# Blank rows written in the mixer, the experts' first rows and weights asked for in attention, four places for weights

## The reference, cut to what matters

```python
x = _layernorm(x + _L0_attn_ref(x, ...))              # a Mamba-2 mixer: projection, conv, scan, gate, projection
x = _layernorm(x + _L0_xattn_ref(x, ctx_1024, ...))   # attention of 16 heads over 77 context rows
x = _layernorm(x + _L0_ffn_ref(x, ...))               # 8 experts, each token to its best 2

def _L0_ffn_ref(x, gate_w, w1, b1, w2, b2, ln_g, ln_b):
    scores = xt @ gate_w
    ew, ei = jax.lax.top_k(scores, K)                 # K = 2, E = 8
    ew = jax.nn.softmax(ew, axis=-1)
    ...
    h = gelu(xt @ w1[e] + b1[e])                      # 256 -> 512
    o = h @ w2[e] + b2[e]                             # 512 -> 256
    y = _layernorm(xt + o, ln_g[e], ln_b[e])
    out = sum over the two experts of ew * y
```

## Time and profile before

| | us |
|---|---|
| median of 3 runs | 2362.49 (2360.77 to 2363.33) |
| the profiled execution, whole | 2369.48 |
| its span, first to last instruction | 2367.7 |
| TensorE busy | 2160.6 (91%) |
| VectorE busy | 1704.4 (72%) |
| ScalarE busy | 1444.5 (61%) |
| GpSimd busy | 1178.9 (50%) |
| moved by DMA | 262.02 MB, of it written to HBM 85.00 MB |

### The profile page before, as it was taken

One profiled execution on the slowest core, in us unless ns is written; L12 is line 12 of the kernel. 1 busy time (PEld: TensorE's weight loads), 2 busy tenths in 40 slices (PEclk: granted clock), 3 DMA queues, 4 the chain that ended last, 5 costly groups with the idle time before them and its releaser, 6 DMA issues. The chain is left out here.

```text
span 2367.7 us, 52943 instructions
## 1 busy us (share of the span) xinstructions
PE 2160.6 (91%) x15740; PEld 1921.0 (81%) x15741; DVE 1704.4 (72%) x4452; ACT 1444.5 (61%) x3032; POOL 1178.9 (50%) x1379
## 2 busy tenths in 40 slices
PE   6999999989896997999999999999958999999968
PEld 5887878878785887888888888888848999999934
DVE  6877777778775334776777677767755898888956
ACT  6777777777775335666666666666634444444425
POOL 2655556555564001343444343434333777777767
PEclk9999999999997998999999999999978999999965
DMA  4111111011110452222222222222226777777648
GB/s 147 49 31 35 36 35 35 31 35 35 35 31 23 169 210 88 72 85 79 78 70 73 73 81 70 73 69 85 83 84 227 232 238 235 237 237 244 226 162 288
DMA packets 167944, 262.02 MB, mean 111 GB/s; under 512 B 25068, under 2 KB 90100, under 8 KB 167860
## 3 DMA queue, kind: packets, MB, share of 16 engines
q1 hardware_dynamic: 153812, 224.26, 30.0%
q0 software_dynamic: 12960, 35.67, 4.0%
q10 hardware_dynamic: 1088, 1.07, 0.1%
HBM read 175.94 MB, written 85.00 MB: 110 GB/s over the span
## 5 line engine op out<-in xcount | busy, mean ns | idle before, releaser
L1551 ACT ACTIVATE b_wk_f<-b_ps_s,b_nmx 128x77 f32<-128x77 f32 x1024 | 233.7, 347 | 16.0 <-DVE b_nmx L1599 16.0
L604 DVE SCALAR_TENSOR_TENSOR a_conv<-a_xc_pad,a_cw,a_conv 128x256 f32<-128x256 f32 x384 | 219.4, 632 | 1.0 <-ACT a_conv L478 1.0
L2038 ACT ACTIVATE c_hid<-c_ps_h,c_b_c 128x256 f32<-128x256 f32 x284 | 111.4, 476 | 175.2 <-PE c_ps_h L114 112.5
L1559 ACT ACTIVATE b_pT<-b_ps_pT 77x1024 f32<-77x1024 f32 x128 | 130.6, 1021 | 142.3 <-PE b_ps_pT L1457 142.3
L112 PE MATMUL c_ps_o<-w,c_h_hi 128*128 x568 | 165.7, 292 | 23.4 <-DVE c_h_lo L2072 23.0
L2167 POOL DMA_INDIRECT made_scratch<-c_o_s,c_to x142 | 153.7, 1082 | 62.6 <-issue 32.5
L1615 DVE TENSOR_TENSOR k_wk_lo<-b_ps_oT,k_wk_lo 128x512 fp32r<-128x512 f32 x128 | 88.0, 687 | 128.5 <-ACT k_wk_lo L1565 128.5
L1542 ACT ACTIVATE b_qT<-b_ps_q,b_bq_s 128x256 f32<-128x256 f32 x256 | 107.5, 471 | 107.4 <-PE b_ps_q L114 106.3
L1843 POOL CAST w<-k_c_f 128x256 f32 (+1 forms) x32 | 14.0, 438 | 312.0 <-DMA k_c_f<-in_c_w 312.0
L112 PE MATMUL c_ps_h<-c_xT_hi,c_w 128*128 128x256 f32 x568 | 167.4, 295 | 0.0
L1445 PE MATMUL b_ps_s<-b_kz,b_qT 128*128 128x154 f32 x1024 | 156.2, 295 | 5.3 <-ACT b_wk_f L1551 5.3
(11 more groups left out here) (285 smaller groups left out, 7688.4 us busy)
## 6 DMA issues: line engine op xcount, KB each, us to landing
c_w<-parts_scratch SPq DMA_DIRECT2D x71, 1024.0 KB
c_xa<-sent_scratch SPq DMA_DIRECT2D x71, 260.0 KB, 4.5
d_got<-made_scratch SPq DMA_DIRECT2D x32, 512.0 KB, 4.9
keys_scratch<-k_k_s SPq DMA_DIRECT2D x8, 1232.0 KB, 4.7
b_kz<-keys_scratch SPq DMA_DIRECT2D x64, 154.0 KB, 2.8
b_vv<-values_scratch SPq DMA_DIRECT2D x32, 308.0 KB
a_xT_f<-in_xT SPq DMA_DIRECT2D x32, 256.0 KB, 3.1
a_x_f<-in_x SPq DMA_DIRECT2D x32, 256.0 KB, 2.7
```

The costliest lines, as they stand in the source:

```text
L604: dve.scalar_tensor_tensor(out=conv[:, m, :], in0=xc_pad[:, m, k:k + L], scalar=cw[:, m, k:k + 1], in1=conv[:, m, :], op0=ALU.mult, op1=AL ...
L1551: last = act.activation(pe_[:, u.par, c, :], s_scores[:, c // (C // GM), c % (C // GM), :], ACT.Exp, bias=nmx[:, u.par, c:c + 1])
L1559: act.activation(pT[:, u.par, :, :], ps_pT[0:LK, :, :], ACT.Copy).then_inc(s_pTc, 1)
L2038: last = act.activation(hid[:, T * m:T * m + T], ps_h[t.par][:, m // 2, T * (m % 2):T * (m % 2) + T], ACT.Gelu, bias=b1_c[:, t.par, m:m + 1])
```

## The change

Four things are altered.

1. **Blank rows.** The blank tile comes from the host as an input, `blank`. The mixer loads it once (item 0) and writes it over the *whole* of `routing.sent`, 271 tiles: with each of the items 0 to 29 three transfers of three tiles, and the last tile after the last step. SyncE then waits in the mixer until all have landed. Attention writes none any more: `fill_ends`, the copy to `free`, `nobody` and the operations on `none` go.
2. **First loads.** A new class `ExpertsHead` holds the places of the experts' rows and first weights, in memory that attention has done with, and the two loads. At the end of attention SyncE waits for the last projection and for the table (`TABLE_STEPS`), asks for weights 0, waits for the scatters, and asks for rows 0, rows 1, weights 1, rows 2, weights 2. The experts' stage begins with the third load ahead.
3. **Four places** for the first weights in place of two, asked for three tiles ahead, and in each step ahead of the rows.
4. **`send` on GpSimd** scatters first and then makes `pw` and `by_expert`. The TOKEN mark and the next count move to `exp_gap`, earlier in the item.

The diff, cut to its core:

```diff
@@ mixer_phase, SyncE
+            tiles, per_item = routing.TILES, 3
+            whole_items = routing.n_blank // (tiles * per_item)
+
+            def blank_rows(b):
+                if b.known() and b.value() == 0:
+                    routing.load_blank(sp)
+                    sp.wait_ge(routing.s_none, 16)
+                if not (b.known() and b.value() >= whole_items):
+                    for i in range(per_item):
+                        routing.blank_rows(sp, (b.value() * per_item + i) * (tiles * L), tiles)
...
-            run_steps(sp, n_seq, [(store, 3), (load_xT_ahead, 0), (load_x, 0), (load_following, 0)], spare=2)
+            run_steps(sp, n_seq, [(store, 3), (load_xT_ahead, 0), (load_x, 0), (load_following, 0), (blank_rows, 2)], spare=2)
+            done = whole_items * per_item * tiles
+            for first in range(done, routing.n_blank):
+                routing.blank_rows(sp, first * L, 1)
+            sp.wait_ge(routing.s_blank, 16 * (whole_items * per_item + routing.n_blank - done))
@@ Routing
+    def load_blank(self, sp):
+        sp.dma_start(self.none[:, :, :], self.blank).then_inc(self.s_none, 16)
+
+    def blank_rows(self, sp, first, tiles):
+        sp.dma_start(self.sent[bass.ds(first, L * tiles), :].rearrange("(k p c) d -> p k (c d)", p=P, c=NT),
+                     self.none[:, :, :].rearrange("p c d -> p (c d)").unsqueeze(1).to_broadcast([P, tiles, NT * WIDE])
+                     ).then_inc(self.s_blank, 16)
@@ ExpertsHead (new)
+    X = 8
+    W = 4
+
+    def __init__(self, nc, ctx, signals, weights, head, places):
+        self.w1 = [w[:, :, :].rearrange("p k n -> p (k n)")[:, 0:MF * 2 * D].rearrange("p (q h n) -> p q h n", q=MF, h=2)
+                   for w in places]
+        spans = ([weights.wk_f[:, :, :].rearrange("p k n -> p (k n)")] * 3 + [weights.w_stage[:, 2, :]] * 3
+                 + [head.c_f[:, :, :].rearrange("p k n -> p (k n)")] * 2)
...
+    def load_w1(self, sp, routing, b1, t):
+        e = sp.value_load(routing.table[0:1, 1, bass.ds(t.value(), 1)], min_val=0, max_val=E - 1)
+        sp.dma_start(self.w1[self.place(t)].rearrange("p k h n -> p k (h n)").bitcast(F32),
+                     routing.parts[bass.ds(MF * e, MF), :, :].rearrange("k p n -> p k n")).then_inc(self.s_w1_in[self.place(t)], 16)
+        sp.dma_start(self.b1_c[:, self.place(t), :], b1[bass.ds(e, 1), :, :].rearrange("o p m -> (o p) m")
+                     ).then_inc(self.s_w1_in[self.place(t)], 16)
+
+    def load_rows(self, sp, routing, t):
+        r = sp.value_load(routing.table[0:1, 0, bass.ds(t.value(), 1)], min_val=0, max_val=routing.sent.shape[0] - L)
+        sp.dma_start(self.xa[t.slot], routing.sent[bass.ds(r, L), :].rearrange("(c p) d -> p c d", p=P)
+                     ).then_inc(self.s_xa_in[t.slot], 16)
@@ attention_phase, SyncE
             sp.wait_ge(s_ahead, 16 * E)
-
-            sp.wait_ge(s_none, 3)
-            for i in range(E - 1):
-                sp.dma_start(tile_rows(E * routing.region + L * i), routing.none[:, :, :]).then_inc(s_blank, 16)
-            fill_ends(sp, 0)
-            sp.wait_ge(s_blank, 16 * (2 * E - 1))
+            sp.wait_ge(s_out, 4 * n_seq)
+            sp.wait_ge(s_tab, TABLE_STEPS)
+            experts_head.load_w1(sp, routing, b1, Item(0, 0, ExpertsHead.X))
+            for par in (0, 1):
+                sp.wait_ge(s_scat[par], 16 * 2 * NT * (n_seq // 2))
+            sp.wait_ge(s_pT, 4 * n_seq)
+            experts_head.load_rows(sp, routing, Item(0, 0, ExpertsHead.X))
+            for i in range(1, 3):
+                experts_head.load_rows(sp, routing, Item(0, i, ExpertsHead.X))
+                experts_head.load_w1(sp, routing, b1, Item(0, i, ExpertsHead.X))
@@ attention_phase, ScalarE and VectorE
-            fill_ends(act, E // 2)
...
-            dve.memset(routing.none[:, :, :], 0.0).then_inc(s_none, 1)
...
-                dve.tensor_copy(routing.free[:, :], base[0:1, :]).then_inc(s_free, 1)
@@ attention_phase, GpSimd
                 pool.tensor_tensor(e2[:, :], euler[:, :], gap[:, :], ALU.pow).then_inc(s_e2, 1)
...
+                pool.tensor_copy(x2_t[:, b.par, :, TOKEN], tok[:, :]).then_inc(s_tok, 1)
+                pool.wait_ge(s_tok, b.count(1, 1))
+                pool.tensor_tensor(tok[:, :], tok[:, :], stride[:, :], ALU.add).then_inc(s_next, 1)
 
             def send(b):
 
                 pool.wait_ge(s_w2, b.count(3, 3))
...
+                for c in range(NT):
+                    for n in range(2):
+                        pool.indirect_dma_start(
+                            routing.sent, bass.IndirectOffsetOnAxis(pos[:, b.par, 2 * c + n:2 * c + n + 1], 0),
+                            x2_t[:, b.par, c, :], None).then_inc(s_scat[b.par], 16)
                 pool.tensor_tensor(pw[:, :, :, :].rearrange("p c n e -> p (c n) e"),
...
@@ experts_phase, SyncE
-                if not t.before(2):
-                    sp.wait_ge(s_h, t.ago(2).count(1, 1))
-                    sp.wait_ge(s_gelu, t.ago(2).count(1, 1))
...
+                if not t.before(head.W):
+                    sp.wait_ge(s_h, t.ago(head.W).count(1, 1))
+                    sp.wait_ge(s_gelu, t.ago(head.W).count(1, 1))
+                head.load_w1(sp, routing, b1, t)
...
-            for i in range(2):
-                load_rows(Item(0, i, X))
-                load_w1(Item(0, i, X))
-            load_rows(Item(0, 2, X))
-            run_steps(sp, n_tiles, [(rows_ahead, 0), (w1_ahead, 0)], spare=3, per=X, peel=8)
+                if not (t.known() and t.value() + 3 >= n_tiles):
+                    load_w1(t.ago(-3))
+
+            run_steps(sp, n_tiles, [(w1_ahead, 0), (rows_ahead, 0)], spare=3, per=X, peel=8)
```

More of the change, by code:

```diff
@@ L914, in __init__ @@
         self.own = sb("own", [P, self.n_tiles])
-        self.free = sb("free", [1, E], I32)
         self.none = sb("none", [P, NT, WIDE])
+        self.s_none, self.s_blank = signals.take("r_none"), signals.take("r_blank")
+        self.n_blank = rows // L
+    TILES = 3
+    def load_blank(self, sp):
[4 more added lines that the diff above has]
+                     ).then_inc(self.s_blank, 16)
 class AttentionWeights:
@@ L980, in low, with place, loaded @@
                           self.wk_hi[:, :, 0:self.weights.DH].bitcast(F32), ALU.subtract).then_inc(self.s_klo, 1)
+class ExpertsHead:
+    X = 8
[5 more added lines that the diff above has]
+                 + [head.c_f[:, :, :].rearrange("p k n -> p (k n)")] * 2)
+        self.xa = [span[:, at * NT * WIDE:(at + 1) * NT * WIDE].rearrange("p (c d) -> p c d", c=NT)
+                   for span, at in zip(spans, (0, 1, 2, 0, 1, 2, 0, 1))]
+        self.b1_c = ctx.enter_context(nc.sbuf_tensor("c_b1_c", [P, self.W, MF], F32))
+        self.s_xa_in = [signals.take(f"c_xa_in{i}") for i in range(self.X)]
+        self.s_w1_in = [signals.take(f"c_w1_in{i}") for i in range(self.W)]
+    def place(self, t):
+        return t.slot % self.W
+    def loaded(self, t):
+        return t.turn * (32 * self.X // self.W) + 32 * (t.slot // self.W) + 32
+    def load_w1(self, sp, routing, b1, t):
[8 more added lines that the diff above has]
+                     ).then_inc(self.s_xa_in[t.slot], 16)
 class Projections:
@@ L1277, in attention_phase @@
         pw = head.c_f[:, 0, 584:616].rearrange("p (j a e) -> p j a e", j=NT, a=2)
-        tok, stride, nobody = (weights.mk[:, 1, 64 + NT * i:64 + NT * i + NT] for i in range(3))
+        tok, stride = (weights.mk[:, 1, 64 + NT * i:64 + NT * i + NT] for i in range(2))
         tn, tc = weights.bq_c, weights.bk_c
@@ L1311, in attention_phase @@
         s_xrb, s_ve, s_rs = (sem(n) for n in ("xrb", "ve", "rs"))
-        s_const, s_made, s_held, s_blank, s_none, s_free, s_init = (
-            sem(n) for n in ("gate_in", "made", "held", "blank", "none", "free", "init"))
-        s_e0, s_tok, s_next, s_pw, s_we, s_tok0, s_e2 = (sem(n) for n in ("e0", "tok", "next", "pw", "we", "tok0", "e2"))
+        s_const, s_made, s_held, s_init = (sem(n) for n in ("gate_in", "made", "held", "init"))
+        s_e0, s_tok, s_next, s_pw, s_we, s_e2 = (sem(n) for n in ("e0", "tok", "next", "pw", "we", "e2"))
         s_scat = [sem("scat0"), sem("scat1")]
@@ L2383, in layouts @@
     parts = c(np.concatenate([ffn["w2"].reshape(E * MF, P, D), w1], axis=2))
+    blank = np.zeros((P, NT, D + 4), np.float32)
+    blank[:, :, TOKEN] = 2 * (x.shape[0] + NT * np.arange(P)[:, None] + np.arange(NT)[None, :])
+    blank[:, :, FIRST] = -1.0
     return {
```

122 lines of the change are left out of this document (49 added, 73 removed).

## The result

The changed kernel takes 2373.24 us as the median of 6 runs (2369.4 to 2375.54), the kernel before 2361.63 beside it (2355.81 to 2365.45): ratio 1.0048, 95% interval 1.0033 to 1.0062. It is **slower by 11.6 us**, half a percent, outside the range of 2352.5 to 2366. Later, beside other kernels on another chip, its ratio was 1.0038 (1.0024 to 1.0052).

What follows compares the result with a forecast made beforehand. The prediction saw stages split by all-engine barriers, each read by itself, with the gain at the barriers. Terms -6.3 - 1.3 + 2.8 = -4.8 us take the median from 2362.49 to 2357.7; likeliest case 2354 to 2361, range 2352.5 to 2366.

Steps and rivals of the forecast that it cites:

- Four places: Experts' stage: first weights asked for three tiles ahead change no transfer's moment; nothing, 1 us as the bound.
- Rows and weights ahead of the barrier: Attention to experts: first loads issued before the barrier start the first product earlier; 6.3 us won, bounds 5.0 and 7.5.
- TensorE's clock: Start of experts' stage: fewer matmuls at the lower clock level; 1.3 us won, bounds -0.4 and +3.
- Blank rows in the mixer: Mixer's 30 items: 72 MB of blank writes fit in the queues' slack and don't slow engines; cost nothing.
- Rival B: Mixer's 30 items: blank writes slow engines or delay a SyncE release, 0.4 us an item, 12 us, 2369.7; chance 0.12.
- The end of the mixer: Barrier from mixer to keys: SyncE waits for the last blank tile to land; 2.8 us lost, bounds 2.4 and 5.2.
- A: End of attention: nine moved issues stall, barrier 3 us later; net -0.5 us, 2362.0, no difference that can be told; chance 0.18.

Runs made afterwards that it cites:

- a_regs_first: Changed kernel with SyncE's table reads in the experts' stage put back ahead of the waits for a free place; 0.9973 of the kernel before, 2359.38 us.
- b_regs_last: Kernel before with SyncE's two table reads in the experts' stage moved behind the waits for a free place; 1.0043 of the kernel before, 2376.39 us.
- after_again: The changed kernel, unchanged, measured and profiled a second time; 1.0038 of the kernel before, 2371.83 us.
- b_mixer_blanks: Kernel before with only the change's blank rows written in the mixer, wait at the mixer's end; 0.9963 of the kernel before, 2359.61 us.
- b_blanks_late: Kernel before with blank rows written in the mixer, their wait at the keys and values stage's end; 0.9984 of the kernel before, 2358.17 us.
- a_loads_behind: Changed kernel with early table reads, the blank rows' wait after keys and values, and nine first loads behind the barrier; 0.9981 of before, 2361.25 us.
- a_both_again: Second run of the changed kernel with both repairs: early table reads, blank rows' wait after keys and values; 0.9987 of before, 2361.24 us.
- a_paced_up: Changed kernel with early table reads, and weights t+2 asked for when tile t's first product ends, not its gelu; 0.9993 of before, 2358.11 us.

## Why the prediction was wrong

**The step that failed** is *Four places*: "The queues see the same transfers at the same moments, and TensorE never waits for weights. Nothing; 1 us as the bound". The second half holds. The first doesn't: each tile's weights leave 0.65 us later behind gelu, since the table is read behind the wait. The term was +13.6 us between the first profiles and +11.4 between the second ones. Undoing the late read in the changed kernel takes away 17.3 us (a_regs_first), and the late read put into the kernel before adds 10.6 (b_regs_last, 486.8 us, for 487.1 in after_again). So within the spread of the profiles the late read is the whole of it. And "TensorE never waits for weights" was the wrong test: the burst's moment counts for the transfer beside it, the scatter, on which GpSimd, VectorE and TensorE wait in turn.

**Rows and weights ahead of the barrier**, -6.3: measured -5.6 (12.53 us from the table for 11.7; the start of the stage 9.94 for 9.2). The size is right and the steps came as described, but the credit is wrong: the prediction gave the gain to the rows that were there, and b_mixer_blanks, b_blanks_late and a_loads_behind show that the blank writes' end gives 4.6 to 4.9 us of it with no load moved, and that the early issues add 0.6 us to it.

**TensorE's clock**, -1.3: the sign was wrong. All 24 first matmuls ran at the lower level, for 19 before, and from first product to first `down` passed 10.91 us for 10.38: +0.5, near the bound of 0.4 that the text gave.

**Blank rows in the mixer**, nothing: right. From its first matmul to its last `x1` it takes 755.4 and 749.5 us in the two profiles of before, 756.4 and 754.6 in those of after, 753.8 in b_mixer_blanks. Rival B's price of 0.4 us an item would be 12 us; one of a few us in all could not be told from this spread.

**The end of the mixer**, +2.8: the barrier came 2.5 us later, from 2.5 us to the last blank tile's landing, as said (2.7 was taken). That the clock would then give 3.4 us back in the keys stage wasn't foreseen, and in a_regs_first it didn't.

**Rivals.** A's stall of the issues didn't come: the last weights are issued 8.29 us behind the table's end, for 7.7 forecast. B had the right side, and with 2369.7 nearly the time, but for a wrong reason: that is luck. The right one was none of the cases: the forecast held the stage's pace for given because the transfers, their bytes and their places' owners were compared, and not the order of instructions on the engine that issues them. One sum is loose as well: the bounds of the three terms added up give 2354.4 to 2363.1, not 2354 to 2361; the time lies above both.

## What to carry to other kernels

Read a helper's diff for the order of reads and waits on the issuing queue: the read of a register that a transfer needs belongs ahead of the wait for the transfer's place. Slack of three tiles in a load doesn't make its moment free; look at which small transfer on a serial chain runs beside it, and try the burst at another moment before trusting that it is hidden. Measure the parts of a change one by one: here the simplest part alone did no worse than all of them with both repairs. Take two profiles of one kernel before explaining a difference of a few us in a stage.

## What the runs showed of the hardware

- A read of one table entry by SyncE, with what belongs to it, puts 0.65 us between a wait and an issue; 0.65 us in each of 68 tiles cost 11 to 17 us of a stage of 476 (b_regs_last, a_regs_first), 8 us by a_both_again against after_again.
- With the burst ahead of gelu's end a tile took 6.4 us for long stretches, then 7.0 to 9.3 for others, with the DMA share falling from 0.75 to 0.54 in a_paced_up. What sets it off is open.
- After waits of one length (2.75 and 2.79 us) TensorE went on at 1.2 GHz in one kernel and at 2.4 in the other. The kernels differ in the 2.5 us for which it stood ahead of the stage (7.3 and 9.8 us); that this decides isn't shown, as a_regs_first waited 9.8 us too and its keys stage took 123.1 us, at a granted clock of 0.95 in that half. The six profiles that stood 7.8 us took 120.9 to 121.3, the three that stood 7.3 took 123.8 to 124.0.
